# One list of a batch's steps dealt anew, and the slots of the routing and early-store chains moved

## The reference

```python
x = x + linear_attention(group_norm(x))       # heads of 32: layer-normed q, k; dots = k^T v; out = q dots / 1024
t = t + softmax_attention(layer_norm(t))      # 8 heads, 1024 x 1024 scores per head, then w_agg and a bias
t = t + experts(layer_norm(t))                # gates = 8 Sinkhorn rounds of t @ gate_weight over (tokens, 8 experts);
                                              # each expert takes its 128 best tokens, times its 256 x 256 matrix
```

## Time and profile before

| | |
|---|---|
| median of 3 runs | 1525.11 us (1524.86 to 1526.01) |
| the profiled execution | 1524.4 us, its span 1520.8 us |
| PE busy | 1343.5 us, 88% of the span |
| DVE, ACT, POOL busy | 1017.4, 864.4, 549.0 us |
| batches 2, 3 and 4, each | 152.0 to 152.2 us |
| batches 0, 5, 6 | 161.5, 162.2, 165.9 us |
| mean granted TensorE clock | 0.947 |

### The profile page before, as it was taken

One profiled execution on the slowest core, in us unless ns is written; L12 is line 12 of the kernel. 1 busy time (PEld: TensorE's weight loads), 2 busy tenths in 40 slices (PEclk: granted clock), 3 DMA queues, 4 the chain that ended last, 5 costly groups with the idle time before them and its releaser, 6 DMA issues.

```text
span 1520.8 us, 29096 instructions
## 1 busy us (share of the span) xinstructions
PE 1343.5 (88%) x10849; PEld 917.5 (60%) x10849; DVE 1017.4 (67%) x2077; ACT 864.4 (57%) x1260; POOL 549.0 (36%) x1126
## 2 busy tenths in 40 slices
PE   4688989999999999999999999899998988887633
PEld 3555566667666766676667666657665656555522
DVE  3416766758575857585758575977789757588781
ACT  1346657667666766676667666566656664342100
POOL 1341620345034503450345034412353046643443
PEclk7999999999999999999999999999999998997666
DMA  2043003600360036003600360027000573433422
GB/s 76 3 127 81 2 29 84 167 15 29 84 167 15 29 84 167 15 29 84 167 15 29 84 167 15 1 72 195 27 1 1 133 216 104 119 118 105 123 73 81
DMA packets 66787, 119.15 MB, mean 78 GB/s; under 512 B 10705, under 2 KB 46546, under 8 KB 66642
## 3 DMA queue, kind: packets, MB, share of 16 engines
q1 hardware_dynamic: 56640, 90.47, 22.1%
q0 software_dynamic: 8960, 26.75, 5.9%
q10 hardware_dynamic: 1042, 0.01, 0.0%
HBM read 29.11 MB, written 33.55 MB: 41 GB/s over the span
## 4 chain that ended last, share of the span: by engine, by line
PE 57%; DVE 24%; issue 7%; ACT 4%; POOL 4%; another core or an unknown queue 2%; DMA 0%; POOLq 0%; DVEq 0%; ACTq 0%
PE shared L962 27%; PE scores L918 11%; PE acc L940 10%; DVE prob_sum L1607 6%; PE acc L937 4%; DVE acc_sb L1581 3%; ACT probs L1209 3%; PE shared L957 2%; DVE bn L1340 2%; PE acc L950 2%; DVE best_i L1513 1%; DVE work L1515 1%; DVE best L1511 1%; DVE bn_x L1393 1%
## 5 line engine op out<-in xcount | busy, mean ns | idle before, releaser
L1209 ACT ACTIVATE probs<-scores 128x1024 f32<-128x1024 f32 x512 | 516.7, 1023 | 180.7 <-PE scores L918 91.7
L918 PE MATMUL scores<-query_stack,key_stack 96*128 96x256 f32 x2048 | 343.3, 308 | 13.9 <-ACT probs L1209 11.3
L1607 DVE TENSOR_TENSOR prob_sum<-prob_sum,probs 128x512 f32<-128x512 f32 x512 | 333.0, 712 | 0.0
L918 PEld LDWEIGHTS scores<-query_stack,key_stack 96*128 96x128 f32 x2048 | 275.3, 190 | 83.8 <-issue 42.3
L940 PE MATMUL acc<-probs,v_all 128*32 128x256 f32 x4096 | 293.2, 390 | 7.0 <-issue 5.3
L1242 POOL TENSOR_TENSOR attn_T<-acc_sb 128x256 f32<-128x256 f32 x56 | 45.7, 817 | 447.0 <-DVE acc_sb L1581 442.9
L962 PE MATMUL shared<-w_sb,chan 128*128 128x512 f32 (+1 forms) x512 | 188.0, 503 | 5.0 <-DVE chan L1417 5.0
L940 PEld LDWEIGHTS acc<-probs,v_all 128*32 128x32 f32 x4096 | 115.8, 110 | 107.3 <-issue 42.4
L962 PEld LDWEIGHTS shared<-w_sb,chan 128*128 128x128 f32 x512 | 92.1, 193 | 67.8 <-issue 63.7
L962 PE MATMUL shared<-chan,w1T 128*128 128x512 f32 x256 | 120.9, 606 | 1.6 <-ACT chan L1137 1.6
L1581 DVE RECIPROCAL acc_sb<-acc_sb 128x256 f32<-128x256 f32 x64 | 111.4, 1741 | 0.0
(11 more groups left out here) (216 smaller groups left out, 2069.0 us busy)
## 6 DMA issues: line engine op xcount, KB each, us to landing
query_stack<-hi SPq DMA_DIRECT2D x120, 128.0 KB, 2.5
key_stack<-hi SPq DMA_DIRECT2D x120, 128.0 KB, 2.5
x_sb<-in_x_dram SPq DMA_DIRECT2D x8, 1024.0 KB, 5.3
out_dram<-resid SPq DMA_DIRECT2D x16, 512.0 KB
tokens_scratch<-resid SPq DMA_DIRECT2D x16, 512.0 KB
tokens_scratch<-rows SPq DMA_DIRECT2D x16, 512.0 KB, 4.7
key_stack<-lo SPq DMA_DIRECT2D x60, 128.0 KB, 2.5
query_stack<-lo SPq DMA_DIRECT2D x60, 128.0 KB, 2.5
```

What stands on the lines that cost most here:

```text
L918: last = pe.matmul(score_ps[u % 2][:, QB * r:QB * (r + 1)], key_stack[stack, HG * g + r, P * kt:P * (kt + 1)], query_stack[stack, HG * g + ...
L1209: act.activation(probs[:, u % PROBS, :], score_ps[u % 2][:, :], ACT.Exp, scale=DH ** -0.5) \
L1607: dve.tensor_tensor(total[:, part], probs[:, (u - 1) % PROBS, part] if kt == 1 else total[:, part], probs[:, u % PROBS, part], ALU.add).th ...
```

## The change

It changes no instruction, no buffer and no count of banks (three before and after). It changes three things in the order in which the engines are given their work: the list in `order` (for all batches), the slots of the Sinkhorn rounds of group 0 in batch 5, and the slots in batch 7 of the selection of group 1 and of the early store.

```diff
@@ order @@
              ("store_stats", 0), ("xT", 1, 1), ("xT", 0, 0), ("agg", 4), ("agg", 5), ("x_stats",), ("agg", 6),
-             ("store_rows", 0), ("gmean",), ("store_rows", 1), ("agg", 7), ("store_rows", 2), ("gvar",),
-             ("store_stats", 1), ("rest", 1), ("z2T", 0), ("store_rows", 3), ("z2T", 1), ("z2T", 2), ("z2T", 3),
-             ("xn", 0), ("gate", 0), ("rest", 2), ("qk0", 0), ("gate", 1), ("store_rows", 4), ("gate", 2),
-             ("store_rows", 5), ("z2T", 4), ("xn", 1), ("qk0", 1), ("store_rows", 6), ("rest", 1), ("gate", 3),
+             ("store_rows", 0), ("rest", 1), ("agg", 7), ("gmean",), ("store_rows", 1), ("store_rows", 2),
+             ("gvar",), ("store_stats", 1), ("z2T", 0), ("store_rows", 3), ("z2T", 1), ("z2T", 2), ("z2T", 3),
+             ("xn", 0), ("gate", 0), ("rest", 2), ("qk0", 0), ("gate", 1), ("store_rows", 4), ("qk0", 1), ("xn", 1),
+             ("gate", 2), ("store_rows", 5), ("z2T", 4), ("rest", 1), ("store_rows", 6), ("qk0", 2), ("gate", 3),
...
-             ("v0", 5), ("qk0", 6), ("head_scale", 0), ("resid", 3), ("resid", 4), ("v0", 6), ("head_scale", 1),
-             ("qk0", 7), ("resid", 5), ("v0", 7), ("head_stats", 1), ("sumv",), ("rest", 1), ("head_scale", 2),
+             ("head_scale", 0), ("resid", 3), ("resid", 4), ("v0", 6), ("qk0", 7), ("head_scale", 1), ("rest", 1),
+             ("resid", 5), ("v0", 7), ("head_stats", 1), ("sumv",), ("head_scale", 2), ("qT", 1, 0), ("qT", 0, 0),
...
@@ add_routing @@
-    plan = {5: spaced(routing, 0, 15.25, 1.8),
+    plan = {5: spaced(routing, 0, 19.75, 1.5),
...
-                (26.5, PAIRS, routing.selection(1)[:34])],
+                (25.0, PAIRS, routing.selection(1)[:34])],
...
-    segments[-2].chains.append((27.25, 32.00, early, segments[-1]))
+    segments[-2].chains.append((25.50, 32.00, early, segments[-1]))
```

More of the change, by code:

```diff
@@ L97, in order @@
-             ("v0", 0), ("z2T", 5), ("z2T", 6), ("qk0", 2), ("store_rows", 7), ("v0", 1), ("gate", 4), ("z2T", 7),
-             ("gate", 5), ("resid", 0), ("qk0", 3), ("v0", 2), ("x_sum",), ("gate", 6), ("v0", 3),
-             ("head_stats", 0), ("qk0", 4), ("qk0", 5), ("gate", 7), ("resid", 1), ("v0", 4), ("resid", 2),
-             ("v0", 5), ("qk0", 6), ("head_scale", 0), ("resid", 3), ("resid", 4), ("v0", 6), ("head_scale", 1),
-             ("qk0", 7), ("resid", 5), ("v0", 7), ("head_stats", 1), ("sumv",), ("rest", 1), ("head_scale", 2),
@@ L102, in order @@
[L102 to L111, removed]
@@ L112, in order @@
-             ("square", 3, 1), ("v", 3), ("norms", 3, 1), ("rest", 2)]
+             ("store_rows", 0), ("rest", 1), ("agg", 7), ("gmean",), ("store_rows", 1), ("store_rows", 2),
+             ("gvar",), ("store_stats", 1), ("z2T", 0), ("store_rows", 3), ("z2T", 1), ("z2T", 2), ("z2T", 3),
+             ("xn", 0), ("gate", 0), ("rest", 2), ("qk0", 0), ("gate", 1), ("store_rows", 4), ("qk0", 1), ("xn", 1),
+             ("gate", 2), ("store_rows", 5), ("z2T", 4), ("rest", 1), ("store_rows", 6), ("qk0", 2), ("gate", 3),
[3 rows of a table added]
@@ new lines, in order @@
+             ("head_scale", 0), ("resid", 3), ("resid", 4), ("v0", 6), ("qk0", 7), ("head_scale", 1), ("rest", 1),
+             ("resid", 5), ("v0", 7), ("head_stats", 1), ("sumv",), ("head_scale", 2), ("qT", 1, 0), ("qT", 0, 0),
+             ("rest", 1.25), ("resid", 6), ("resid", 7), ("head_scale", 3), ("rest", 1.5), ("qT", 1, 1), ("dots",),
+             ("lin", 0), ("qT", 0, 1), ("lin", 1), ("lin", 2), ("lin", 3), ("rest", 1), ("front_stats", 0),
+             ("rest", 2.25), ("lin", 4), ("lin", 5), ("lin", 6), ("lin", 7), ("front_stats", 1), ("front_rows", 0),
@@ new lines, in order @@
+             ("front_rows", 1), ("front_rows", 2), ("rest", 1), ("front_rows", 3), ("rest", 0.25), ("zT", 1, 0),
+             ("zT", 0, 0), ("front_rows", 4), ("proj", 0, 0), ("proj", 1, 0), ("square", 0, 0), ("proj", 2, 0),
+             ("norms", 0, 0), ("square", 1, 0), ("front_rows", 5), ("front_rows", 6), ("front_rows", 7),
+             ("proj", 3, 0), ("norms", 1, 0), ("square", 2, 0), ("zT", 0, 1), ("zT", 1, 1), ("norms", 2, 0),
+             ("square", 3, 0), ("proj", 0, 1), ("proj", 1, 1), ("rest", 0.5), ("norms", 3, 0), ("square", 0, 1),
@@ L113, in order @@
+             ("v", 0), ("norms", 0, 1), ("square", 1, 1), ("v", 1), ("norms", 1, 1), ("proj", 2, 1), ("v", 2),
+             ("square", 2, 1), ("proj", 3, 1), ("norms", 2, 1), ("square", 3, 1), ("v", 3), ("norms", 3, 1),
+             ("rest", 2)]
     wanted = {"store": store, "attend": attend, "front": front, "rest": attend and front}
```

## The result

The changed kernel took 1502.45 us (median of 4 runs, 1501.53 to 1503.60), the kernel before beside it 1524.99 (4 runs); the ratio is 0.9851, 95% interval 0.9835 to 0.9867. The change wins 22.5 us; the forecast was 10.3, and the range began at 1507.5. The direction was right, the size was not, and no rival had it.

What follows compares the result with a forecast made beforehand. TensorE (PE), busy 88% of the span, was taken as the bound. Six middle batches' 7.8 plus batch 0's 3.0 less the rounds' 0.5 gave 10.3 us won: median 1514.8 us, 8-in-10 range 1507.5 to 1522.5.

Steps and rivals of the forecast that it cites:

- At most 2.1 us of such a batch can be won by any order: Middle batches of 152.0 us: PE is busy 149.9, so reordering steps can win only the remaining idle time.
- Slots 2 to 8: Batches 1 to 6: gmean and gvar one slot later, qk0.1 earlier; 0.6 us won by the start of slot 8.
- at nothing: Slots 8 to 11: same steps dealt otherwise with PE full, priced at zero; some 0.5 us if banks come late.
- The cover: Slots 6 and 7: PE work including early qk0.1 hides the late exponential; without it 0.9 us lost instead of 0.6 won.
- Slots 12 to 17: v0.7, head_stats.1 and sumv one slot later: PE's slot 15 stall goes, POOL's chain takes 6.4 us; 0.7 us won.
- the rival with 13 slow links: Slots 12 to 17: every POOL link slowed by DVE adds, middle-batch gains given back, total 1522.6 us; chance 0.12.
- Batch 0: Slots 1 to 4: gmean, gvar and xn.0 later, totals no longer hang on POOL; 3.0 us won, bounds 0 and 5.3.
- Batch 5, the rounds: Eight Sinkhorn rounds moved to slot 19.75 every 1.5: cost 10.7 us against 10.2, so 0.5 lost.
- the 7.7 named: Batch 5: forecast called wrong if slots 19 to 23 take over 7.7 us more than those of batch 4.
- Batch 6: Counted as one of six middle batches, winning 0.6 + 0.7 = 1.3 us.
- DVE's work is only spread ... I take 0, bounds 3 either way: Batch 7 and behind: earlier selection and early store only spread DVE's work, gathers rule; 0 us, bounds 3 either way.

Runs made afterwards that it cites:

- h2: Changed kernel with store_rows.4 back in the first half of slot 6, ahead of the second exponential, qk0.1 kept early; middle batch 154.03 us.
- i1: Changed kernel with qk0.1 and xn.1 back in slot 7, both row steps behind slot 6's second exponential, z2T.4 behind qk0.1; middle batch 150.45 us.
- f4: Kernel before with the new list up to v0.1 only, qk0.1 and xn.1 left behind z2T.4; batches 2 to 4 took 156.8 to 156.9 us.
- g1: Kernel before with the new list only behind head_stats.0, other slots as before; batches 1 to 4 took 152.15, 151.85, 151.56 and 151.53 us.
- e1b: Kernel before with the new step list alone, measured again on a later occasion; ratio to the kernel before 0.9898.
- c2: Changed kernel with batch 5's Sinkhorn rounds put back at slot 15.25 every 1.8; ratio to the kernel before 0.9867.
- a3: Changed kernel with the early store of batch 7 put back at slot 27.25; ratio to the kernel before 0.9903.
- e1: Kernel before with the new step list alone, rounds and late slots of batch 7 as before; ratio to the kernel before 0.9915.
- e4: Kernel before with the new step list and the selection of group 1 from slot 25.0, early store still from 27.25; ratio 0.9897.
- s2: Kernel before with only the early store of batch 7 moved, to slot 25.50; ratio to the kernel before 0.9982.
- s1: Kernel before with only the selection of group 1 moved, to slot 25.0 of batch 7; ratio to the kernel before 0.9998.

## Why the prediction was right, and where it was wrong

In short: the middle batches were won by the mechanism described, for a reason that was only half seen, and the step that failed by most is the last term of the sum, batch 7 and what lies behind it, put at 0 and measured at 8.6 us.

**What bounds the kernel: right.** "At most 2.1 us of such a batch can be won by any order": 2.0 were won, and the middle batch is now 150.03 us with PE busy 149.34. This bound was the better forecast of the middle batches than my sum. It is not exact: PE's busy time itself fell by 0.5 (from 149.88). And the batches with all three parts and no routing are four, 1 to 4, not five; the sum is not touched by it.

**Slots 2 to 8: the mechanism right, the size 0.6 for 1.0, and the cost "at nothing" behind it 0.5 for nothing.** In the old count slot 4 starts at 593.17 (forecast 593.4), slot 8 at 608.83 (forecast 609.2) against 609.83 before. Over slots 8 and 9, "the same steps dealt a little otherwise", PE takes 12.09 us (603.34 to 615.43) and before 12.60 (609.83 to 622.43), with the same steps done at the end of both but for a row step. The timelines list no wait of PE there. Start to start, the scores of the two slots take 1.36 us each before and 1.04 and 1.15 after, which is the whole difference; all other steps add up to 9.88 and 9.90. Why the scores take less behind the new order of steps is not settled.

**The cover: wrong, in the sentence "Without that cover it would be 0.9 lost".** I followed one POOL chain, gvar's, to xn.0, the adds and the exponential, and named qk0.1 as what hides it. The second chain, store_stats.1, is queued behind the first on POOL and ends at 600.5 in the changed kernel's own time; what waits for it is a row step on ACT with an exponential behind it, and z2T.4 on PE with four groups of weighing behind it. h2 and i1 part the two: the place of the row step is worth 4.0 us, that of qk0.1 0.4; i1, without the cover, is still 1.6 us better than before. The change works because store_rows.4 crosses the middle of slot 6, which I listed in the table of dealt slots and gave no price. That the sum of these slots was nevertheless near is luck: the cover that I named moves the right step along with it. And a stall can cost more than its length: f4's 3.47 us made slot 7 longer by 6.2 (11.24 - 5.07).

**Slots 12 to 17: right** (-0.7 forecast; g1 -0.5 in batch 3, and -0.7 in slot 15 with 0.2 given back in slot 17). The chain took 7.4 us, not 6.4. The count of slow links was right: links 1 to 4 and 6 to 9 take 0.56 to 0.65 us, links 5 and 10 to 13 take 0.24 to 0.32, eight and five. What I left out are the gaps of some 0.08 us between one link's end and the next one's start, 12 of them, which make the missing 1.0. The rule of the Trainium skill (SBUF — State Buffer, "Who interferes with whom") fits the rows: the slow links lie beside the adds of 637.64 to 640.39 and 640.71 to 643.51, four adds of 0.69 us in each stretch and four links beside them, one link an add; link 5 starts in the gap, at 640.58, and the last four behind the adds. What kept the rival with 13 slow links away is that the adds do not last as long as the chain.

**Batch 0: -3.0 forecast, -1.3 measured, and it varies.** At slot 4 the changed kernel is 1.8 us ahead (forecast 3.0), in slots 5 to 9 3.4 to 3.7: PE's 3.67 at the totals is gone, with 1.96 at gvar in its place. Then 1.8 us go in slots 14 and 15; at the start of slot 23 the lead is 4.4 again, and slot 23 takes 3.0 of it. Windows there of the changed kernel:

```profile
175.60:191.60 16.00, 13.52 (x110) 9.43 (x110) 9.22 (x11) 6.64 (x8) 5.06 (x5) 0.79 0.01 2
216.30:226.30 10.00, 9.30 (x63) 5.37 (x64) 2.83 (x6) 5.69 (x8) 3.81 (x13) 0.83 0.12 40
```

Before, the same slots have a clock of 0.88 (14.20 us) and 1.00 (7.00 us). Of the 1.8 us lost PE's busy time makes up 1.6, of the 3.0 it makes up 2.3, over the same matmuls. The same batch of the changed kernel took 160.19, 163.76 and 161.62 us on three occasions, that of the other kernels with the new list, which is the same there, 160.2 (e1b, c2, a3) and 161.7 to 161.8 (e1, e4), and that of kernels with the old list 161.4 to 161.7 in five profiles. So in half of the eight profiles nothing is won. The term that failed is the one I did not have: the clock that PE is granted in this batch.

**Batch 5, the rounds: about right.** 10.7 forecast for the new slots, 10.2 measured (160.21 - 150.03). That the old slots would still cost 10.2 under the new list was wrong: 11.2 (161.20 - 150.0). So the rounds won 1.0 where I had 0.5 lost. Slots 19 to 23 take 6.4 us more than those of batch 4, under the 7.7 named.

**Batch 6: -1.3 forecast, -3.3 measured.** I counted it as one of six middle batches. But DVE's selection makes its slots 13 to 21 longer than a middle batch's: slots 15 and 16 took 8.86 us before and 5.78 after. The first part of the list wins nothing there: slot 8 starts, from the batch's start, 0.5 us later than before. g1 alone has 162.28 us, so the gain lies in the second part of the list. In three other profiles the new list gave 164.1 to 164.3 (-1.8).

**"DVE's work is only spread ... I take 0, bounds 3 either way": the main miss, 8.6 of the 13 us.** Two things stand behind it. The early store, dealt from slot 25.5 on, wins 2.7 us (s2) or 2.2 to 3.5 (a3), by measurements that are hardly clear of noise; the selection wins nothing that s1 could see. It was not DVE's work alone that moved: both moves take work out of what follows slot 30 of batch 7, a stretch that takes 40.3 us in the mean with both and 45.3 with neither, of which some is given back before it. What the runs of the late slots show as won, up to 3.5 us, is little more than my bound of 3. The other 5 to 6 us lie in the same stretch: the profile of before was the slowest of eighteen there (48.6 us at clock 0.77, the next 45.7) and that of the changed kernel within 0.1 us of the fastest (39.2 at 0.88). The list alone won 12.9 and 15.3 us on its two occasions (intervals of 4 and 2 us to either side), 12.4 of them before batch 7 starts. On the later occasions slots 0 to 23 of batch 7, where I had seen nothing to win, take 98.4 to 100.0 us in the nine profiles with the first part of the new list and 100.7 to 103.1 in the three with the old one; on the first occasion they took 118.3 before and 118.4 after. The whole was worth 22.5, 20.1 and 18.0 us on three occasions, with intervals of 20.3 to 25.2, 17.1 to 23.3 and 15.3 to 20.5, which just meet. Whether the first was really more, and why, when both kernels repeated within 2 us, stays open; all that the parts explain is 18.

## What to carry to other kernels

Where a step moves on an in-order engine, price what is queued second behind it as well: here the chain that gained a slot was covered, and the next chain on the same engine decided. To a stall of TensorE add what the clock may take: where the granted clock fell behind them, waits of 1.85, 2.09 and 3.47 us put the start of slot 9 off by 4.0, 4.0 and 6.3 us against the changed kernel; where it did not fall, a wait of 1.86 us cost 2.5. When the busy share of the bounding engine says that 2.1 us can be won and the steps add up to 1.3, the difference may be a term that has been given no price; the range should reach to the bound.

## What the runs showed that I had not expected

**The same kernel is 20 us faster on some occasions, all of it in batch 7.** The list-only kernel took 1506 us in one comparison and 1483 in a later one, with the kernel before at 1522 and 1499. Both were taken on the chip numbered 4. Windows of batch 7, to its slot 30, in its two profiles, the earlier first, and then the group of POOL's scatters in each (busy, mean ns of one, idle before by releaser):

```profile
1193.79:1350.60 156.81, 137.29 (x1197) 97.91 (x1193) 107.64 (x245) 80.54 (x109) 82.83 (x104) 0.95 0.49 146
```

```profile
1193.91:1326.85 132.94, 125.68 (x1196) 93.42 (x1193) 106.79 (x245) 80.22 (x108) 82.25 (x104) 1.00 0.58 172
```

```profile
L1319 POOL DMA_INDIRECT out_dram<-chan,slot_token x12 | 15.1, 1257 | 19.2 <-DVE chan L1551 14.5 <-issue 4.4 <-DVE x_sb L1551 0.3
```

```profile
L1319 POOL DMA_INDIRECT out_dram<-chan,slot_token x12 | 13.3, 1106 | 6.1 <-DVE chan L1551 3.0 <-issue 2.7 <-DMA out_dram<-chan,slot_token 0.3
```

The scatters wait 14.5 us for the gathered and multiplied rows on the one occasion and 3.0 on the other; PE's granted clock is 0.95 and 1.00. Batches 2 to 4 agree to 0.1 us (149.98, and 150.01 to 150.03). Before it copies the transposed rows of a gather (L1192), ACT waits 16.7 us in four places for something outside the engines on the first occasion, and nowhere on the second. That points at the gathers, served faster on some occasions; that it is they is not shown, and neither is why.

**A short chain on POOL takes 6.2 or 8.0 us.** The chain of store_stats.1, on tiles of 4 columns, ran from 597.15 to 603.37 before and runs from 592.51 to 600.50 after: behind the first two, of 0.52 and 0.34 us, its links take 0.20 us up to 594.9 and 0.40 to 0.79 from there on, beside two groups of four adds, 2.43 and 2.48 us, on DVE. Before, four of its links behind the first took over 0.5 us, after, eight. This is the second reason, beside its later start, why the row step that needs it came late in f4.
